# Scan with the step size inside the decay: one product of 32 rows per half chunk, and its sums spread by VectorE at places 7 and 3

## The reference

```python
Acs = jnp.cumsum(Ac, axis=-1)                       # Ac = dt * A, per chunk and head
Ldec = jnp.where(tri, jnp.exp(Acs[..., :, None] - Acs[..., None, :]), 0.0)
Y_diag = jnp.einsum('bcqhn,bcshn,bhcqs,bcshp->bcqhp', Cc, Bc, Ldec, Xc)   # Xc = xs * dt
decay_states = jnp.exp(Acs[..., -1:] - Acs)
states = jnp.einsum('bcqhn,bhcq,bcqhp->bchpn', Bc, decay_states, Xc)
Y_off = jnp.einsum('bcqhn,bchpn,bhcq->bcqhp', Cc, prev, jnp.exp(Acs))
```

## Time and profile before

| | |
|---|---|
| median of 3 runs | 2383.64 us (2360.32 to 2384.04) |
| profiled execution | 2373.73 us, span 2372.0 us |
| PE busy in the span | 2151.1 us, 91% |
| DVE, ACT, POOL busy | 1654.6, 1266.2, 1526.2 us |
| scan, first to last chunk's start | 84.36 to 695.46 us |
| granted TensorE clock, mean | 0.935 of full |

### The profile page before, as it was taken

One profiled execution on the slowest core, in us unless ns is written; L12 is line 12 of the kernel. 1 busy time (PEld: TensorE's weight loads), 2 busy tenths in 40 slices (PEclk: granted clock), 3 DMA queues, 4 the chain that ended last, 5 costly groups with the idle time before them and its releaser, 6 DMA issues. The chain is left out here.

```text
span 2372.0 us, 39890 instructions
## 1 busy us (share of the span) xinstructions
PE 2151.1 (91%) x11907; PEld 1749.7 (74%) x11907; DVE 1654.6 (70%) x4242; ACT 1266.2 (53%) x2623; POOL 1526.2 (64%) x1473
## 2 busy tenths in 40 slices
PE   4799998999995999999999999999999993799993
PEld 2466666666674888888888888888888882688883
DVE  4778976877846677777877878778777773344444
ACT  3556555555531666666666666666666661233331
POOL 2678866866841666677686785867868675355551
PEclk9988988898885999999999999999999996899995
DMA  1950000000000001010010010100101001455555
GB/s 62 387 185 10 10 10 1 10 1 1 1 19 19 10 1 26 1 27 18 4 41 1 11 35 1 43 2 8 37 1 41 5 7 41 171 191 189 198 170 213
DMA packets 135401, 130.93 MB, mean 55 GB/s; under 512 B 82885, under 2 KB 101359, under 8 KB 135190
## 3 DMA queue, kind: packets, MB, share of 16 engines
q1 hardware_dynamic: 124950, 107.12, 14.8%
q0 software_dynamic: 9088, 17.07, 2.1%
q10 hardware_dynamic: 1152, 4.19, 0.4%
HBM read 64.78 MB, written 65.10 MB: 55 GB/s over the span
## 5 line engine op out<-in xcount | busy, mean ns | idle before, releaser
L1219 POOL TENSOR_TENSOR plo<-pf,phi 128x512 fp32r<-128x512 f32 (+1 forms) x640 | 752.0, 1187 | 340.2 <-ACT phi L1447 311.2
L1445 ACT ACTIVATE pf<-psum 128x512 f32<-128x512 f32 (+1 forms) x640 | 357.1, 558 | 412.9 <-PE psum L1280 310.6
L1447 ACT ACTIVATE phi<-psum 128x512 fp32r<-128x512 f32 (+1 forms) x640 | 355.1, 555 | 0.0
L1591 DVE CUSTOM_DVE_ANT_0 psum<-psum,ahead_wide 128x128 f32<-128x128 f32 (+3 forms) x512 | 246.8, 503 | 70.1 <-PE psum L1333 68.5
L1278 PE MATMUL psum<-phi,x_tok 128*128 128x512 f32 (+1 forms) x640 | 265.8, 415 | 5.8 <-POOL plo L1219 5.8
L1872 POOL DMA_INDIRECT chosen<-yg,xg x156 | 152.8, 979 | 154.2 <-DVE yg L1984 109.3
L1333 PE MATMUL psum<-xT,qT 128*128 128x512 f32 (+3 forms) x768 | 246.0, 349 | 3.8 <-DVE peak L1591 3.4
L1278 PE MATMUL psum<-qT,xT 128*128 128x512 f32 (+1 forms) x640 | 238.1, 372 | 1.1 <-DMA qT<-nmax 0.6
L1279 PE MATMUL psum<-plo,x_tok 128*128 128x512 f32 (+1 forms) x640 | 237.6, 371 | 0.0
L1280 PE MATMUL psum<-phi,x_tok 128*128 128x512 f32 (+1 forms) x640 | 237.4, 371 | 0.0
L1279 PE MATMUL psum<-qT,xT 128*128 128x512 f32 (+1 forms) x640 | 236.8, 370 | 0.0
(11 more groups left out here) (291 smaller groups left out, 5306.3 us busy)
## 6 DMA issues: line engine op xcount, KB each, us to landing
wg<-turned_w SPq DMA_DIRECT2D x39, 874.0 KB, 4.6
routed<-empty SPq DMA_DIRECT2D x1, 34056.0 KB, 95.8
xg<-routed SPq DMA_DIRECT2D x39, 264.0 KB, 4.2
qT<-nmax SPq DMA_DIRECT2D x512, 0.5 KB, 2.0
y<-chosen SPq DMA_DIRECT2D x8, 1024.0 KB, 10.2
turned_w<-wT SPq DMA_DIRECT2D x8, 874.0 KB, 4.5
x_in_sb<-in_x SPq DMA_DIRECT2D x8, 512.0 KB, 3.3
out<-o_st ACTq DMA_DIRECT2D x8, 512.0 KB, 5.7
```

The source lines that it names most:

```text
L1219: g_.tensor_tensor(plo[:, T % RP, 0:n], pf[:, T % RF, 0:n], phi[:, T % RP, 0:n].bitcast(F32), ALU.subtract).then_inc(a["low_ready"], 1)
L1445: s_.activation(pf[:, T % RF, 0:n], bank[T % RS][:, 0:n], ACT.Exp)
L1447: s_.activation(phi[:, T % RP, 0:n], bank[T % RS][:, 0:n], ACT.Exp).then_inc(a["high_ready"], 1)
L1591: last = v.tensor_tensor_reduce(out=source[:, col:col + n], in0=source[:, col:col + n], in1=ahead_wide[:, HALF - n:HALF], scale=1.0, scala ...
```

## The change

The difference that goes into the exponential gets the logarithm of the step size at the key added, so that Ldec and to_end hold dt already, and xdt is no longer made: y uses `tok` and Xd is tok times to_end. The sums of a chunk (query and key, each as a high and a low part, for 8 heads: 32 rows) are brought into partitions by `turn_sums` on PE, with two products each for two halves of an image; `high_sums` (ACT) and `split_sums` (DVE) part them, `set_sums` (ACT) makes the key side `by_key` and `at_query`, and `spread_sums` (DVE) spreads at_query over the 8 heads to `by_query`, four chunks at a time, at places 7 and 3. Then `chunk_seg` needs the mask product and one product with 32 rows per half. One tap moves from place 5 to place 4 in DVE's table; `normalise` moves from place 6 to 5, the first `turn_back` of place 6 in front of the turn of y, and `spread_bc` of place 7 in front of the first pad_copy. bcs is no longer a tile of its own. The diff, cut to its core:

```diff
                     def chunk_end(g):
-                        pool.wait_ge(s["xdt_ready"], g + 1)
+                        pool.wait_ge(s["tok_copied"], g + 1)
-                                         xdt[:, g % 2, :].rearrange("p (h d) -> p h d", d=HD),
+                                         tok[:, g % 4, 0:DI].rearrange("p (h d) -> p h d", d=HD),
...
-                        if 0 <= step < G:
-                            chunk_in(step)
...
+                    def turn_sums(n):
+                        spare_free("sums_low", n + 1)
+                        pe.wait_ge(s["log_less"], n + 1)
+                        for half in range(2):
+                            to = spare[:, half * P:(half + 1) * P]
+                            t.matmul(to, dA[:, 4 * half:4 * half + 4, :, :].rearrange("p c k h -> p (c k h)"), upto[:, :], start=True, stop=False)
+                            last = t.matmul(to, less_log_flat[:, half, :], ident[:, :], start=False, stop=True)
+                        last.then_inc(s["sums_turned"], 1)
...
                     def chunk_seg(g):
-                        if c == 0:
-                            pe.wait_ge(s["sums_apart"], n + 1)
+                        if c % 4 == 0:
+                            pe.wait_ge(s["sums_set"], n + 1)
+                            pe.wait_ge(s["sums_spread"], 2 * n + c // 4 + 1)
+                        mine = slice(32 * (c % 4), 32 * (c % 4) + 32)
...
-                            t.matmul(seg, halves[:, n % 2, :], minus_one[:, c, 4 * j:4 * j + 4].unsqueeze(2).to_broadcast([P, 4, P]),
-                                     start=False, stop=False)
-                            last = t.matmul(seg, group_ones[:, 2 * c + j:2 * c + j + 1].to_broadcast([P, P]), apart[:, n % 2, :, :], start=False, stop=True)
+                            last = t.matmul(seg, by_key[mine, n % 2, c // 4, :], by_query[mine, c // 4, 4 * j:4 * j + 4, :], start=False, stop=True)
...
+                    def log_of_steps(n):
+                        act.wait_ge(s["dA_ready"], n + 1)
+                        need(act, "log_less", n)
+                        a_.activation(log_dt[:, :], dt[:, n % 2, :], ACT.Ln, bias=least[:, 0:1]).then_inc(s["log_ready"], 1)
+
+                    def high_sums(n):
+                        act.wait_ge(s["sums_turned"], n + 1)
+                        a_.activation(sum_high.bitcast(F32R), spare[:, 0:2 * P].rearrange("p (a q) -> p a q", q=P), ACT.Copy).then_inc(s["sums_high"], 1)
+
+                    def set_sums(n):
+                        act.wait_ge(s["sums_split"], n + 1)
+                        need(act, "sums_spread", 2 * n)
+                        need(act, "seg_ready", (n - 1) * NC)
+                        a_.activation(at_query[:, :, :], sum_part, ACT.Identity, scale=is_query[:, 0:1], bias=not_key[:, 0:1])
+                        a_.activation(by_key[:, n % 2, :, :], sum_part, ACT.Identity, scale=is_key[:, 0:1], bias=is_query[:, 0:1]
+                                      ).then_inc(s["sums_set"], 1)
...
+                    def spread_sums(n, half):
+                        dve.wait_ge(s["sums_set"], n + 1)
+                        need(dve, "seg_ready", (n - 1) * NC + 4 * (half + 1))
+                        v.tensor_tensor(by_query[:, half, :, :], at_query[:, half, :].unsqueeze(1).to_broadcast([P, NH, P]),
+                                         of_head[:, :].unsqueeze(2).to_broadcast([P, NH, P]), ALU.mult).then_inc(s["sums_spread"], 1)
...
-                               4: ((1, range(1, 3)),), 5: ((1, range(3, 6)),), 6: ((1, range(6, 9)),)}
+                               4: ((1, range(1, 4)),), 5: ((1, range(4, 6)),), 6: ((1, range(6, 9)),)}
```

More of the change, by code:

```diff
@@ L549, in _ @@
                                 project_z(n - 1, 3)
-                        if has(nn) and j == 2:
-                            residual(nn, 0)
+                        if has(nn):
+                            if j == 2:
+                                residual(nn, 0)
+                            if j == 6:
+                                turn_back(nn, 0)
                         if 3 <= step < G + 6:
@@ L577, in _ @@
                                 project(n, 5)
+                            if j == 4:
+                                turn_sums(n)
                         if has(nn):
@@ L756, in _ @@
                                 soft_plus(n)
+                            if j == 2:
+                                log_of_steps(n)
+                            if j == 5:
+                                set_sums(n)
                             if j == 4:
@@ L764, in _ @@
                                 tanh_bc(n)
[L765 to L766 removed]
                         if has(n) and j == 7:
                             spread_bc(n)
+                        if has(nn):
+                            if j == 5:
+                                normalise(nn, 0)
+                                normalise(nn, 1)
+                            if j == 7:
+                                pad_copy(nn, 0)
                         if 0 <= step - 2 < G:
@@ L775, in _ @@
                                 pad_copy(n, 5)
+                            if j == 4:
+                                high_sums(n)
                         if has(nn):
@@ L956, in _ @@
                                 step_sizes(n)
+                            if j == 3:
+                                logs(n)
                             if j == 4:
                                 cumulated(n)
+                            if j == 5:
+                                split_sums(n)
                         if has(nn) and j == 3:
@@ L971, in _ @@
                             chunk_lnx(step - 5)
-                        if has(n) and j == 6:
-                            sums_apart(n)
                         if has(n - 1):
@@ L978, in _ @@
                                 gate_z(n - 1, 3)
+                        if has(n - 1) and j == 3:
+                            spread_sums(n - 1, 1)
                         if has(n):
+                            if j == 7:
+                                spread_sums(n, 0)
                             if j == 5:
```

133 lines of the change are left out of this document (67 added, 66 removed).

## The result

The changed kernel takes 2478.3 us (median of 4 runs, 2442.1 to 2482.0), the kernel before 2381.3 (2360.3 to 2384.0). The ratio is 1.035 with a 95% interval of 1.019 to 1.051: slower by 97 us by the medians and by some 83 us by the ratio, where 2380 was forecast and 2425 was the upper end. The ratio leaves out the two slower runs of the changed kernel (2479.1 and 2482.0 us) and rests on the other two, 2477.5 and 2442.1, which is why its interval is wide. The four runs show mean granted clocks of 0.889 to 0.906, and the one at 0.906 is the 2442. The profiled execution took 2477.5 us with a span of 2475.1.

What follows compares the result with a forecast made beforehand. PE was taken as near its limit in the last image, with waits elsewhere and VectorE equally full in places 3 to 5. First two images +5.6, next five -6, last -3.6: 2383.6 - 4 = 2380 us, range 2343 to 2425.

Steps and rivals of the forecast that it cites:

- One product fewer per half: In each chunk's two halves on PE: dropping the 0.24 us third product saves 0.45 us a chunk, 29 us over 64.
- Rival D: A 32-row product takes as long as the two it replaces, so the 0.45 gains are lost: 2390 us, chance 0.05.
- The clock: Scan's granted clock stays at 0.88; PE slows behind idle time, as line 523 did after a 1.60 us wait.
- rival B: Spreads queue behind POOL and idle time before turn_sums lowers the clock: +7.3 us for seven images, 2431 us, chance 0.18.
- Place 3: Logarithm on ACT (0.3 us, table loads 1.28) delays project_z; PE idles some 2.2 us, place 4 starts at 271.2 against 270.77.
- Place 4, the spread: VectorE's spread takes 1.22 us (bounds 1.22 and 3.2), and PE waits 1.4 us for it.
- The end of place 4: Before turn_sums PE idles 3.4 us for VectorE's gate, then four products take 1.6 us; place 5 starts 5.0 later.
- rival C: No new wait binds, and 29 us of products plus the old waits come back: 2329 us, chance 0.05.
- Places 5 to 7: Place 5 takes 7.1 or 8.6 us, place 6 13; place 7 changes by +0.3 (spread +1.22, earlier BC -0.9).

Runs made afterwards that it cites:

- after: The changed kernel itself, with the mask product and one 32-row product per half, against the kernel before: 2478.3 us, ratio 1.035.
- e11: Changed kernel with the mask's product also over 32 rows, the same rows as the product behind it: 2453.3 us, ratio 1.035.
- e1: Changed kernel with the product of line 491 over all 128 rows instead of 32: 2380.1 us, ratio 1.005.
- e6: Kernel before with its 32-row products (lines 468, 469, 526) over 128 rows, BC and S padded with zeros: 2344.9 us, ratio 0.991.
- e4: Changed kernel with the whole preparation of the sums made for the first image alone: 2482.1 us (2431.3 to 2494.2).
- e12: Changed kernel with the product of line 491 over 64 rows instead of 32: 2455.4 us, ratio 1.037.
- e3: Changed kernel with the mask's 128-row product issued twice in each half: 2451.1 us, ratio 1.032.
- e2: Kernel before with its product on halves (line 479) over 32 of the 128 rows: 2496.6 us, ratio 1.046.
- e7: Changed kernel with line 491 over 128 rows, by_key zero outside the first chunk's rows, and BC and S zero-padded: 2363.5 us, ratio 0.997.
- e5: Changed kernel with line 491 over 128 rows and by_key zero outside the first chunk's 32 rows: 2382.8 us, ratio 1.007.

## Why the prediction was wrong, point by point

**What the loss is made of.** Two effects, neither of them a term of the prediction. The changes of row count cost 0.57 us a chunk at the full clock (1.49 in after against 0.92 with all rows, two halves of 0.46), 36 us over 64 chunks. The rest is the low clock: e11, which has no change inside a half, still has 1.035 where e1 has 1.005, 3.0% or 72 us. How the loss of the changed kernel itself divides isn't settled. By ratio e11 and after don't differ (1.030 to 1.040 and 1.019 to 1.051), and e11 isn't after without the gaps, since its mask product has 32 rows too and can lower the clock by itself.

**"One product fewer per half" failed, and it is the step that carried everything.** It took 0.24 us from the row of a 128-row product among 128-row products and applied it to a step whose new product has 32. The step has become 0.14 us a chunk longer, not 0.45 shorter: 0.59 us a chunk, 38 us over the scan, was mis-sized at the full clock. With all rows the gain is there, 0.43 a chunk (1.35 to 0.92). Rival D, "a 32-row product takes as long as the two it replaces", came nearest to this, with 2390 us and a chance of 0.05; even it was too mild, since two products with one of 32 rows take 0.745 us where the three took 0.68. It was dismissed by a row of a 128-row product, which says nothing on it. The kernel before had rows that did: its own 32-row products (line 469 and its neighbours) stand between full ones in every chunk, and e6 shows what they cost.
The Trainium skill's page "TensorEngine Tiling (Array Packing)" (Key Properties) says that changing the tiling mode drains the TensorE. The page doesn't say that a plain product of 32 rows is such a change. If it is, the 0.28 us between the starts of lines 490 and 491 that vanish with one row count are that price. The prediction did not weigh this rule, and it should have.

**The clock.** The prediction treated the low clock as something that follows idle time, which is what its rows showed: 1.45 for line 523 behind a wait of 1.60. It forecast 0.88 for the scan, and 0.80 for rival B through a wait of more than 1.6 us. Measured is 0.74, and in stretches without any wait. That is the second step that failed: a low clock was priced only behind idle time, and here it came with few rows at work and PE fully busy. B's sign was right and its mechanism was not: e4 takes the new waits away and stays between 2431 and 2494.

**Place 3.** The logarithm took 0.35 us behind a load of 1.28, as forecast. The logarithm starts 1.30 behind the load's start, so the drain that the Trainium skill's page "ScalarE: Activation LUTs" (What ACT_TABLE_LOAD costs) adds isn't in these rows either. The logs on VectorE took 1.57, not 0.42, while an add of taps ran on POOL beside them. PE's wait for project_z, forecast at 2.2 us an image, isn't there: its line 462 has no idle time in after, and 3.8 us in the whole scan of e1.

**Place 4, the spread.** Line 921 has its 1.22 (median 1.218, one at 3.2), between the bounds and at the value taken. PE's wait was 2.18 in the second image where 1.4 was forecast: the spread ended at 225.96, 2.94 into the place, because VectorE's round came late; the logs alone are 1.15 of it.

**The end of place 4.** Not 3.4 us of idle time seven times, but 0.49 in the second image and 5.4 in the whole scan. VectorE's gate came nearly where it was put (12.1 us into the place, 11.4 forecast), but PE was through with its products only 11.7 in, where 8.0 was forecast: it had waited for the spread and then run at the low clock. In e1, where the clock holds better, it is 7.3 us in seven images, about 1 each. By the prediction's own test ("under 1 us, C") this is nearer to rival C than to the forecast, though the time is nowhere near C's. The four products took 0.99 us (235.22 to 236.21) and not 1.6: the 0.41 was read from one product with another kind behind it, where here four of one kind follow each other. Place 4 of the second image was 13.19 us long all the same, with spread, turned sums and some slow clock.

**Places 5 to 7.** Place 5 took 7.89 and 7.99 us against 7.1 to 8.6 forecast: right. Place 6 took 12.56 in the third image against 13: right, and Xd waits only 6.6 us in the whole scan. Place 7 took 14.47 with PE busy throughout at 0.63, against 12.7: the clock.

**The preparation, with the rows repaired.** Here the rest of the sum can be judged. In e1 the 28 us of shorter products are there and the preparation takes 39 back, ratio 1.005, where the prediction had a balance too, of -4 us (0.998). The balance was sound in kind; its largest terms, the waits at project_z (2.2 us an image) and at turn_sums (3.4), came to 3.8 and 7.3 us in the whole scan and make up 11 of the 39. That e1's median is 2380.1 like the forecast is chance: the kernel before stood at 2371.6 in that set.

**What stays open.** How the clock is decided: e12 (0.79) and e3 (0.84) lie between after and the kernels with all rows, and no run gives the rule. Why a change costs 0.28 us for the pair at line 491, 0.38 in e2, and 0.13 and 0.20 in e6's two places isn't known either. In which terms the other 19 of the 39 us lie isn't settled. A changed kernel with zero-padded keys and the reference's output wasn't run; it would need four times the keys, and e7 without that cost is already slower than e6.

## What to carry to other kernels

A product's price on TensorE isn't only its columns: one with fewer rows than its neighbours paid 0.13 to 0.38 us here for the change there and back, and with such products in every half the clock fell for everything around them, with PE fully busy. Before replacing two full products by one narrow one, look in the trace for a narrow one between full ones and take its start-to-start times, not the duration of a full one. Where the buffer has room, pad with zeros: e6 did it to three small products of the kernel before and took 0.9% off the time.

## What the hardware showed that was not expected

- The granted clock fell to 0.50 with PE busy 79.44 of 79.44 us (e11, last image). With the same count of products over 128 rows (e1) images 2 to 8 had 0.86, and 0.83 with zeros in 96 rows of the key side (e5).
- Rows of zeros count as rows: ratio 1.007 with 96 of the key's 128 rows zero (e5), 1.005 with numbers in them (e1).
- 64 rows pay the same for the change as 32: 0.745 us a half in both, 0.46 with 128, and 0.45 where both products have 32 (e11).
- Adding 28 us of work didn't make the kernel slower (e3 1.032, after 1.035): the clock was 0.84 against 0.74.
